# Transposes of the softmax weights two steps behind their scores in an attention, FFN and mixture-of-experts kernel

## What is computed

```python
c = einsum(x, W[itok]) + b[itok]                      # per sequence
Q, K, V = heads(c @ W_Q), heads(c @ W_K), heads(c @ W_V)
scores = einsum('bhqd,bhkd->bhqk', Q, K) / 4 + causal
probs = softmax(scores)
x = x + einsum('bhqk,bhkd->bhqd', probs, V) @ W_o     # x1
h = relu(x @ wi.T + low-rank) @ wo.T + low-rank       # FFN
gate = softmax(h @ gate_w + gate_b); top2 = top_k(gate, 2)
out = x + sum over top2 of gate * expert(h)           # gelu, gelu, linear
```

## Time and profile before

| | us |
|---|---|
| median of 3 runs | 1537.2 |
| lowest, highest | 1536.48, 1538.39 |
| the profiled execution | 1538.85 |
| its span | 1537.3 |

### The profile page before, as it was taken

The page is one execution under the profiler, slowest core; times in us unless marked ns, Lnnn a source line. Parts: engine busy times, 40 slices in busy tenths (PEclk is TensorE's granted clock), DMA queues, the critical chain, the costliest instruction groups (busy, mean ns, idle before and its releaser), DMA issues.

```text
span 1537.3 us, 31909 instructions
## 1 busy us (share of the span) xinstructions
PE 1416.1 (92%) x10169; PEld 1085.2 (71%) x10170; DVE 864.5 (56%) x1927; ACT 764.6 (50%) x2000; POOL 419.1 (27%) x553
## 2 busy tenths in 40 slices
PE   6989999999999999999999998339999999999997
PEld 3556776776776776776776776237878888888886
DVE  2665665665665665665664663464555555555554
ACT  3675665665665665665664663003333333333332
POOL 2222211211211211221221220033344544444442
PEclk9599999999999999999999999659999999999998
DMA  6121222222222222222222220381624222442221
GB/s 237 62 83 56 77 84 90 77 84 90 77 84 90 77 84 90 76 84 90 77 84 69 77 78 28 158 332 35 230 58 142 43 40 50 138 145 40 40 38 13
DMA packets 50642, 138.62 MB, mean 90 GB/s; under 512 B 10515, under 2 KB 29587, under 8 KB 48755
## 3 DMA queue, kind: packets, MB, share of 16 engines
q0 software_dynamic: 28992, 68.35, 16.2%
q1 hardware_dynamic: 21554, 68.97, 12.1%
HBM read 86.82 MB, written 51.38 MB: 90 GB/s over the span
## 4 chain that ended last, share of the span: by engine, by line
PE 83%; DVE 5%; DMA 4%; ACT 3%; issue 3%; POOL 1%; POOLq 0%; SPq 0%; DVEq 0%; ACTq 0%
PE bank L651 68%; PE bank L802 10%; PE bank L895 4%; ACT probs L1060 2%; DMA xg<-hrows,gid 1%; PE bank L887 1%; DMA wsplit<-w_rest 1%; DMA out<-y_sb,sid 1%; DVE nmax L1238 1%; DMA w_rest<-in_w_all 1%; PE bank L810 0%; DVE probs_t L1252 0%; POOL hit_v L1496 0%; ACT w_high L961 0%; POOL w_rest L1476 0%
## 5 line engine op out<-in xcount | busy, mean ns | idle before, releaser
L1060 ACT ACTIVATE probs<-bank,nmax 128x512 f32<-128x512 f32 (+3 forms) x512 | 266.0, 525 | 171.0 <-DVE nmax L1238 169.5
L1238 DVE TENSOR_REDUCE nmax<-bank 128x1 f32<-128x512 f32 (+3 forms) x512 | 227.3, 486 | 209.3 <-PE bank L651 209.0
L1094 ACT ACTIVATE g<-z 128x512 f32<-128x512 f32 x142 | 89.8, 632 | 279.5 <-DVE z L1426 279.5
L1476 POOL TENSOR_TENSOR w_rest<-w_rest,w_high 128x512 f32<-128x512 f32 x64 | 81.4, 1271 | 467.7 <-ACT w_high L961 467.7
L802 PE MATMUL bank<-id_f,probs 128*128 128x128 f32 x1280 | 202.9, 290 | 0.2
L651 PE MATMUL bank<-wst,g1t_high 128*128 x568 | 185.3, 407 | 0.9 <-DVE g1t_low L1414 0.9
L802 PEld LDWEIGHTS bank<-id_f,probs 128*128 128x128 f32 x1280 | 138.4, 143 | 44.0 <-issue 27.0
L1518 POOL DMA_INDIRECT out<-y_sb,sid x71 | 114.3, 1609 | 150.1 <-DVE y_sb L1447 69.1
L1252 DVE COPY probs_t<-bank 128x128 f32<-128x128 f32 (+3 forms) x320 | 140.3, 454 | 9.1 <-PE bank L802 9.1
L1426 DVE TENSOR_TENSOR z<-bank,b_sb 128x512 f32<-128x512 f32 x142 | 98.2, 691 | 72.5 <-PE bank L651 61.1
L651 PEld LDWEIGHTS bank<-wst,g1t_high 128*128 128x128 f32 x568 | 102.2, 190 | 20.8 <-issue 1.1
(11 more groups left out here) (193 smaller groups left out, 2921.2 us busy)
## 6 DMA issues: line engine op xcount, KB each, us to landing
wst<-wsplit SPq DMA_DIRECT2D x8, 4096.0 KB, 12.5
w_rest<-in_w_all POOLq DMA_DIRECT2D x64, 256.0 KB, 3.0
wsplit<-w_high POOLq DMA_DIRECT2D x64, 256.0 KB, 2.3
wsplit<-w_rest POOLq DMA_DIRECT2D x64, 256.0 KB, 2.6
hrows<-h_sb SPq DMA_DIRECT2D x8, 528.0 KB, 3.0
x_in<-in_xT SPq DMA_DIRECT2D x8, 512.0 KB, 3.5
wb_raw<-in_lora_wb SPq DMA_DIRECT2D x8, 512.0 KB, 3.5
x_res<-in_xT SPq DMA_DIRECT2D x8, 512.0 KB, 3.3
```

The costliest lines, as they stand in the source:

```text
L1060: taken(nc.scalar.activation(probs[:, s % 4, 0:(i + 1) * P], at(n, rd)[:, 0:(i + 1) * P], ACT.Exp, bias=nmax[:, s % 8:s % 8 + 1], accum_ou ...
L1094: nc.scalar.activation(g[:, :], z[:, :], ACT.Gelu).then_inc(s_g, 1)
L1238: V.tensor_reduce(nmax[:, s % 8:s % 8 + 1], at(n, rd)[:, 0:(s // HEADS + 1) * P], AX.X, ALU.max, negate=True).then_inc(s_max, 1)
L1476: nc.gpsimd.tensor_tensor(w_rest[:, :], w_rest[:, :], w_high[:, :].bitcast(F32), ALU.subtract).then_inc(s_wlow, 1)
```

## The change

The transposes of a unit come two steps behind its scores (`T_LAG` 2), the product with V three (`PV_LAG` 3), and `ot_sb` four steps behind the tile's last scores (`NORM_LAG` 4). `rinv` and rt keep their distance of one and two steps. `probs` gets six slots, which lengthens the space kept for it in SBUF. `STEPS` follows `NORM_LAG` and becomes 36, so the list of fillers gets an empty entry: step 8, the first of tile 1, has no filler, and every later filler comes one step later than before.

```diff
-T_LAG, PV_LAG = 1, 2
-INV_LAG, RT_LAG, NORM_LAG = 1, 2, 3
+T_LAG, PV_LAG = 2, 3
+INV_LAG, RT_LAG, NORM_LAG = 1, 2, 4
 STEPS = UNITS // PAIR + NORM_LAG
+PROB_SLOTS = 6
+BEHIND = PT_SLOTS + PROB_SLOTS - 8
 FILLERS = ([(("hid", j), k) for j in range(HID_EARLY, KF) for k in range(KD)] +
-           [(("x1", t2), 0) for t2 in range(TB // 2)] + [(("low_o", 0), 0)] +
+           [(None, 0)] + [(("x1", t2), 0) for t2 in range(TB // 2)] + [(("low_o", 0), 0)] +
-            probs = sb("probs", [P, 4, S], F32, attn)
+            probs = sb("probs", [P, PROB_SLOTS, S], F32, attn)
-        behind_attn = sb("behind_attn", [P, PT_SLOTS - 4, S], F32)
+        behind_attn = sb("behind_attn", [P, BEHIND, S], F32)
-        weight_space = sb("weight_space", [P, 2 * W_ALL - (PT_SLOTS - 4) * S], F32)
+        weight_space = sb("weight_space", [P, 2 * W_ALL - BEHIND * S], F32)
-                                                      probs[:, t % 4, kb * P:(kb + 1) * P], id_f[:, :])
+                                                      probs[:, t % PROB_SLOTS, kb * P:(kb + 1) * P], id_f[:, :])
-                        taken(nc.scalar.activation(probs[:, s % 4, 0:(i + 1) * P], at(n, rd)[:, 0:(i + 1) * P], ACT.Exp,
+                        taken(nc.scalar.activation(probs[:, s % PROB_SLOTS, 0:(i + 1) * P], at(n, rd)[:, 0:(i + 1) * P], ACT.Exp,
```

## The result

The changed kernel takes 1549.6 us (median of 7 runs, 1546.3 to 1557.0) against 1537.2 us (7 runs, 1531.3 to 1541.1). The ratio is 1.0091 with a 95% interval of 1.0067 to 1.0115, that is 14 us more (10 to 18); the medians are 12.4 us apart. Forecast were 5.8 us more: the sign was right, and the time lay inside the whole range of 1535 to 1551, but the size was less than half of what was measured.

A forecast was written before the change was run, and what follows sets the result against it. TensorE was taken to bound the attention rounds, so only its waits and its clock could matter. Terms A -1.4, B +0.7, C +12, D -1.5, E -4 sum to +5.8 us on 1537.2, 1543.0 us; own range 1538 to 1549, whole range 1535 to 1551.

The forecast's parts named there:

- C: Steps 9, 17, 25: masks behind rt wait for score banks, no product with V hiding it; 1.7 us a round, +12 us.
- A: End of a round: the wait for `rrep` becomes a shorter one for `ht_sb`; 0.2 us less in seven rounds, -1.4 us.
- D: Step 25, rounds 0 and 4: step 24's product with V covers most of the mask wait from late casts; -1.5 us.
- B: Round 0, without FFN: eight more end transposes and rt's turns cost, less work at half clock gains; +0.7 us.
- E: Openings of rounds: shifted round ends make three or four of six long clock falls short; -4 us, from -7 to +1.
- Rival 3: Round ends: the clock falls earlier, ahead of the last transposes, slowing these, rt and gate; 1551 us, chance 0.12.
- Rival 1: Round ends: shifted falls all become short, so the clock gives C's loss back; 1538 us, chance 0.15.
- Rival 2: Behind rt: TensorE doesn't wait as VectorE and ScalarE run ahead, nor does the gate; 1530 us, chance 0.10.
- Rival 4: Whole kernel: the change does nothing, waits only change places; 1537 us, chance 0.08.

## Why the prediction was right in sign and wrong in size

**What bounds the kernel** was read rightly: the lag's aim was a wait that isn't there, and TensorE's standing still and its clock are what counted.

**C, the products with V.** Forecast +1.7 us a round. The scores of step 31 come 99.93 us behind the first `ot_sb` product and came at 100.02 before, though eight transposes (0.92 us of TensorE's time) and a `next` product (0.86) have moved behind them: 1.7 us lost. The term holds in size. Its split doesn't. The masks wait 1.22 us a round and not 0.39, 0.8 more where 1.7 were forecast; 0.3 more is rt's wait for `rrep` in step 9, which C had at nothing; the last 0.5 us is spread over transposes and products that start a little later, and its cause stays open. The run with rt one step later takes 1.0 us off up to the last scores, but not the wait at step 10.

**A, the end of a round.** Forecast -0.2 us. From the last scores to the opening it is 820.15 - 808.57 = 11.58 us, and was 460.17 - 450.75 = 9.42 (the scores at 450.75 in the trace of before). Less the 1.8 us that moved there, +0.4 and not -0.2. The step that failed is "`rrep` is done while eight more transposes and a `next` product run". The wait for `rrep` went, but I let the transposes behind the last scores run at 1.09 us a group. With one `next` product between two groups, the second waits for the copies of the first: it starts 0.26 us late and takes 0.32 us more, 0.6 in all. A was forecast at -1.4 us and came to +2.8.

**D, late casts.** Forecast -1.5 us, and in round 4 it became a loss. The product with V of step 24 does stand ahead of the masks of step 25, and the second of them still waits, ahead of rt as in the earlier trace rows. In the changed kernel:

```profile
553.46 0.62 ACT L963 CAST w_high<-w_rest 128x512 fp32r<-128x512 f32 x1 [3.14 <-DMA w_rest<-in_w_all]
...
554.81 0.29 PE L653 MATMUL bank<-mask_b,id_b 128*128 128x128 bf16 x1 [2.06 <-ACT probs L1062]
```

The same cast before:

```profile
548.41 0.62 ACT L961 CAST w_high<-w_rest 128x512 fp32r<-128x512 f32 x1 [2.11 <-DMA w_rest<-in_w_all]
```

D took the cast's lateness as fixed. ScalarE stood 3.14 us in front of it and not 2.11, since its transfer landed later against the work. Why it did is open. The masks of round 4 wait 2.84 us in all, 1.6 more than those of its neighbours; before it was 1.55, 1.2 more.

**B, round 0.** Forecast +0.7 us, range -1.5 to +3. Round 1's first `ot_sb` product comes at 118.8 and 116.2 us in the two traces of before and at 115.3 and 117.8 after. The two traces of one kernel differ by more than the term, by how long the low stretch lasts.

**E, the clock.** Forecast -4 us, and this is the larger miss. From the `ot_sb` product of round 1 to that of the last opening it is 804.1 us before and 818.0 after, 13.8 more, of which six rounds of 1.8 us, 2.2 for round 7 and 0.4 for D take 13.4. So E is between 0 and +1 in the first pair of traces, and 802.4 against 821.2 makes it +5 in the second, both good to about 1 us, since a few other rounds of the kernel before have late exponentials too. The step that failed is "With rounds of another length the points shift, and some falls will be short ones". They did become short, but I counted only falls at round ends. The clock also fell at the waits of 0.2 to 0.3 us in steps 9 and 10, one of which is new, at the late cast of round 4, and behind the wait for `k_sb`, which both kernels have, and a fall inside a round cost 1.5 us.

**The rule on transposes.** The Trainium skill ("TensorE: Matmul & The Clock Gate", Part 4: PE-mode transpose) has transposes not count as busy in the same way as products. Rival 3, which follows from its full form, didn't happen: at the end of round 2 with the empty filler the clock stays full through 12 us that hold 20 of these transposes (the row 330 to 342 above), and no round end of the changed kernel reads below 0.72. The low clock of round 0, which the prediction took as agreeing with the rule, is no support for it: in the second trace of the kernel before the same steps run at 1.00. The Trainium skill ("TensorE: Matmul & The Clock Gate", Part 1: The HAM clock gate) says that the activity monitor runs on freely and doesn't start anew with the kernel. That agrees with the falls of two traces of one kernel standing in different places.

**Rivals.** Rival 1 had each fall become short, and the time go back; they became short and the time didn't, as new ones came. Rival 2 fell with the rows of the masks. Rival 4 is refuted by the ratio.

**The prediction's own sums.** The forecast itself adds up. Three sums beside it don't: rival 1 with C at +8 to +9 comes to about -1 us, 1536 to 1537 and not 1538; rival 2 leaves out B and E, with which it would be near 1527; and the range "with C from +8 to +16 and E from -7 to +1" runs from 1536 to 1552 and not from 1538 to 1549. That the measured median lies inside the whole range is partly luck. In the first pair of traces rounds 1 to 7 are 13.8 us longer, but round 0 ends 3.5 us sooner, with 20 us at low clock and not 38, so the span is only 10.2 us longer; between the two second traces it is 19.4.

What stays open: how much of the run with transposes one step behind (ratio 1.0042) against the changed kernel (1.0091) is waits and how much is clock, since its fall-free round is known only with a fall taken off; why the weight transfer of round 4 landed later; and what decides whether the clock falls in a given stretch, which differed between two traces of one kernel.

## What to carry to other kernels

When a lag is changed, list what keeps its old distance: here the transposes of the sums and the gate stayed and lost the work that had covered them. They cost some 2 us a round, the lag itself at most 0.2. A stretch in which TensorE does little is paid twice, once in waits and again in the clock of the dense work behind it, so put the dense product into such a stretch and the narrow ones where dense work surrounds them. And before a term for the clock is given a sign, look at every place with short waits, not only at those where it falls in the one trace at hand.

## What the runs showed of the hardware that was not expected

- The time at low clock isn't a property of the program: round 0 of one program was low until 77 us in one trace and until 63 us in another, and round ends had falls of 6.8 or 3.4 us or none at equal waits.
- With waits of 0.99 and 0.75 us around gate products of 8 columns and a product with V that fills 32 output rows, the clock fell at the ends of rounds 1 to 6 in both traces of the kernel before. In the changed kernel, with waits of 0.88 and 0.76 us there, it fell at five of six, and at one of six with two products of 512 columns in these waits.
- One more step with an empty filler, which does no work, made the kernel 0.8% faster at step 8 and 1.4% at step 27, the larger part of it through the clock.
